# Two graph-attention layers on one core: row lists moved ahead, pair steps moved back, five adjacency gathers in flight

## What is computed

```python
# layer 0
att    = ((x[sub] @ Wq.T + bq) * (x[obj] @ Wk.T + bk)) summed over each of 8 heads / sqrt(64)
scores = zeros(8, n, n); scores[:, sub, obj] = att
scores = where(adj == 0, -inf, scores); scores[:, i, i] = 1e-07
x = layernorm(x + mean_over_heads(softmax(scores)) @ x)
# layer 1
seq = (x @ W_seq) in 16 heads
hidden = softmax(leaky_relu(s1[i] + s2[j]) masked by adj) @ seq
x = layernorm(x + elu(hidden @ W_out + b_out))
```

## Time and profile before

| what | value |
|---|---|
| median of 3 runs | 434.89 us (434.27 to 435.85) |
| the profiled execution's own time | 433.42 us |
| its span in the profile | 431.1 us |
| PE (TensorE) busy | 351.7 us, 82% |
| DVE (VectorE) busy | 323.1 us, 75% |
| ACT (ScalarE) busy | 202.1 us, 47% |
| POOL (GpSimd) busy | 186.5 us, 43% |

### The profile page before, as it was taken

The page is one execution under the profiler, slowest core; times in us unless marked ns, Lnnn a source line. Parts: engine busy times, 40 slices in busy tenths (PEclk is TensorE's granted clock), DMA queues, the critical chain, the costliest instruction groups (busy, mean ns, idle before and its releaser), DMA issues.

```text
span 431.1 us, 5195 instructions
## 1 busy us (share of the span) xinstructions
PE 351.7 (82%) x1650; PEld 214.2 (50%) x1650; DVE 323.1 (75%) x813; ACT 202.1 (47%) x451; POOL 186.5 (43%) x180
## 2 busy tenths in 40 slices
PE   1599999999600699979999999258898999999991
PEld 1155644544300354537887877036554565565650
DVE  0999799766500556977777785778799999999955
ACT  3867664476200021225564534211154477577684
POOL 6655767655367100000000000677778887884000
PEclk9999999999955699999999999578999999999997
DMA  7999144436940013219311111575666567666014
GB/s 263 380 390 378 37 176 126 156 112 161 276 123 0 6 48 74 99 25 365 120 58 52 68 59 52 154 216 140 176 190 187 153 198 225 180 201 193 24 51 152
DMA packets 34758, 65.11 MB, mean 151 GB/s; under 512 B 15648, under 2 KB 16800, under 8 KB 32672
## 3 DMA queue, kind: packets, MB, share of 16 engines
q1 hardware_dynamic: 25632, 42.45, 28.9%
q0 software_dynamic: 9088, 22.20, 18.8%
HBM read 53.50 MB, written 8.52 MB: 144 GB/s over the span
## 4 chain that ended last, share of the span: by engine, by line
DVE 32%; DMA 22%; PE 19%; POOL 15%; issue 7%; ACT 3%; another core or an unknown queue 0%; DVEq 0%; POOLq 0%; SPq 0%
DMA pr<-in_adj_dram,aidx 21%; PE ps L811 12%; POOL pr L524 8%; DVE adjT L1939 8%; POOL adjT L603 6%; PE ps L633 3%; DVE arenaC L1806 2%; DVE ps L1864 2%; DVE adjT L1804 2%; DVE ps L1857 2%; DVE arenaA L1870 2%; DVE stage L1929 2%; PE ps L800 2%; PE ps L671 2%; DMA adjT<-seqtab,eidx 1%
## 5 line engine op out<-in xcount | busy, mean ns | idle before, releaser
L633 PE MATMUL ps<-arenaB,adjT 128*128 128x512 f16 x512 | 120.2, 392 | 5.5 <-ACT adjT L982 3.2
L524 POOL DMA_INDIRECT pr<-in_adj_dram,aidx x79 | 83.1, 1051 | 52.5 <-DMA pr<-in_adj_dram,aidx 36.1
L603 POOL DMA_INDIRECT adjT<-seqtab,eidx x64 | 76.1, 1189 | 19.5 <-issue 19.5
L633 PEld LDWEIGHTS ps<-arenaB,adjT 128*128 128x128 f16 x512 | 50.2, 101 | 66.8 <-issue 6.3
L925 PE MATMUL ps<-adjT,stage 128*128 128x264 f32 x256 | 67.1, 409 | 18.5 <-DVE adjT L1939 11.5
L603 POOL DMA_INDIRECT adjT<-seqtab,near x16 | 21.2, 1322 | 126.2 <-DMA seqtab<-arenaA 120.3
L925 PEld LDWEIGHTS ps<-adjT,stage 128*128 128x128 f32 x256 | 48.8, 198 | 41.1 <-DVE ps L1864 16.5
L811 PE MATMUL ps<-stage 128*128 128x272 f32 x256 | 61.5, 394 | 0.2 <-ACT stage L1068 0.2
L838 PE MATMUL ps<-adjT 128*128 128x512 f32 x120 | 54.1, 593 | 1.0 <-issue 1.0
L811 PEld LDWEIGHTS ps<-stage 128*128 128x128 f32 x256 | 47.4, 190 | 9.6 <-ACT stage L1068 0.8
L1939 DVE TENSOR_TENSOR adjT<-adjT 128x1024 f32<-128x1024 f32 (+2 forms) x35 | 47.8, 1371 | 1.9 <-issue 1.3
(11 more groups left out here) (274 smaller groups left out, 507.6 us busy)
## 6 DMA issues: line engine op xcount, KB each, us to landing
stage<-in_adj_dram SPq DMA_DIRECT2D x16, 1024.0 KB
seqtab<-arenaA SPq DMA_DIRECT2D x16, 264.0 KB, 2.0
arenaA<-in_x_dram SPq DMA_DIRECT2D x4, 1024.0 KB, 12.1
out_dram<-arenaC SPq DMA_DIRECT2D x16, 256.0 KB
arenaB<-in_x_dram SPq DMA_DIRECT2D x1, 1536.0 KB, 10.4
pr<-in_adj_dram,aidx POOLq DMA_INDIRECT x79
arenaC<-in_L_gnn_Wq_dram SPq DMA_DIRECT2D x1, 1024.0 KB
arenaC<-in_L_gnn_Wk_dram SPq DMA_DIRECT2D x1, 1024.0 KB
```

The costliest lines, as they stand in the source:

```text
L524: g.indirect_dma_start(out=avals[:, t:t + 1], out_offset=None, in_=adj_flat, in_offset=bass.IndirectOffsetOnAxis(ap=aidx[:, t:t + 1], axis ...
L603: g.indirect_dma_start(out=Grow[:, b % GR, k, :], out_offset=None, in_=seqtab, in_offset=bass.IndirectOffsetOnAxis(ap=source, axis=0)).the ...
L633: ins = t.matmul(bank(4 + b % 2), adjT[:, b, j, :], xsplit[:, w, j, :], start=(j == 0 and w == 0), stop=(j == NB - 1 and w == 1))
```

## The change

- GpSimd: from gather 24 on (`CALM`) five may be in flight (`FLIGHT`), before it three as before. The mask `nearer` is made by VectorE at its start, and is 64 wide.
- TensorE: `pair_offsets` and `pair_list` move from block 11 to block 13, `pair_turn` and `pair_qk` from 12 to 14, `count_rows` and `pair_rows` ahead of block 15, `pair_sums` and `pe_sum_flags` to its middle. Blocks 0 and 1 are multiplied quarter by quarter side by side.
- VectorE: the list of block 13 is finished before `count_pairs`; those of 14 and 15 stand between `fetch_pairs` and the branch. In the arm, `all_listed` comes before `attend`, and `lone_rows` and `measure` before `weigh_pairs`. Block 0's list comes before the first `low`.
- ScalarE: the cast of block 15 moves ahead of the branch. SP: block 1 is loaded before the first quarter of `x`, block 2 before the last.
- The tables of the pair steps are 64 wide where they were 128 (at most 64 pairs are taken in this arm). `attend` waits for q and for k apart.

The diff, without its renamings:

```diff
-    FLIGHT = 3
+    FLIGHT = 5
+    CALM = 24
-        diag = part(stage, 2176, [10, P])
-        prod8 = part(stage, 2176, [H0, P])
+        diag = part(stage, 2176, [10, FEWER])
+        prod8 = part(stage, 2176, [H0, FEWER])
...
             load_row(0)
+            load_row(1)
             load_x(0)
-            load_row(1)
             load_x(1)
             load_x(2)
+            load_row(2)
             load_x(3)
-            load_row(2)
...
             for t in range(T):
-                if t >= FLIGHT:
-                    pool.wait_ge(c_av[t % FLIGHT], 16 * (t // FLIGHT))
+                ahead = FLIGHT if t >= CALM else 3
+                if t >= ahead:
+                    pool.wait_ge(c_av[(t - ahead) % FLIGHT], 16 * ((t - ahead) // FLIGHT + 1))
...
-                if b == 11:
+                if b == 13:
                     pair_offsets()
+                if b == 14:
+                    pair_qk()
                 multiply(b, 2 * Q, 3 * Q)
-                if b == 11:
+                if b == 13:
                     pair_list()
...
+            count_rows()
+            pair_rows()
             multiply(NB - 1, 0, Q)
             multiply(NB - 1, Q, 2 * Q)
             pe_sum_flags()
+            pair_sums()
+            multiply(NB - 1, 2 * Q, 3 * Q)
             pair_scatter()
-            multiply(NB - 1, 2 * Q, 3 * Q)
...
-            list_keys(NB - 3)
+            listing(NB - 3)
             count_pairs()
             place_pairs()
             fetch_pairs()
-            list_top(NB - 3)
+            listing(NB - 2)
+            listing(NB - 1)

             def last_rows():
-                listing(NB - 2)
+                all_listed()
                 attend()
-                listing(NB - 1)
-                all_listed()
-                weigh_pairs()
                 lone_rows()
                 measure()
+                weigh_pairs()
                 share_pairs()
                 weigh_rows()
```

More of the change, by code:

```diff
@@ L243, in two_layer_graph_attention @@
         pair_step = Stage(sem("pair_step"), ["tot", "hot8", "cur", "diag", "mx8", "akeep", "vsel"])
+        pair_pe = Stage(sem("pair_pe"), ["off", "list", "turn", "q", "k", "cnt", "rows", "bad", "sums", "scat"])
         A_dve = Stage(sem("A_dve"), [f"hot{c}" for c in range(NCH)] + ["shift", "so", "idx", "prod", "red", "att",
@@ L993, in _ @@
                 if q == 0:
-                    save_turned(0)
-                if q == 1:
-                    cast_row(1)
-            save_turned(1)
-            cast_row(2)
+                    save_turned(1)
+                if q == 2:
+                    cast_row(2)
+            save_turned(2)
+            for b in range(2):
+                save_ax(b)
+            cast_row(3)
             def block_step(b):
@@ L1011, in block_step @@
                         s.copy(WT[:, g // KT, g % KT, :], bank(6 + g % 2)).then_inc(w_evac_a, 1)
-                if b == 13:
-                    act.wait_ge(so_turned, 1)
+                if b == 14:
+                    act.wait_ge(pair_pe.sem, pair_pe.after(0, "turn"))
                     for w in range(2):
@@ L1017, in last_rows @@
             def last_rows():
-                for b in (NB - 2, NB - 1):
-                    block_step(b)
+                block_step(NB - 1)
+                act.wait_ge(pair_pe.sem, pair_pe.after(0, "rows"))
+                s.copy(Up[:], ps[:, 1, 0:P]).then_inc(u_saved, 1)
                 act.wait_ge(pair_step.sem, pair_step.after(0, "mx8"))
@@ L1025, in last_rows @@
                 save_ax(NB - 2)
-            for b in range(2, NB - 2):
+            for b in range(3, NB - 1):
                 block_step(b)
@@ L1346, in fetch_pairs @@
             def fetch_pairs():
-                dve.wait_ge(listed8, 1)
+                dve.wait_ge(pair_pe.sem, pair_pe.after(0, "list"))
                 link(v.tensor_scalar_add(cur[:, 0:2], ps[:, 7, 0:2], -1.0))
@@ L1448, in weigh_rows @@
                                        ALU.subtract).then_inc(fast_done, 1)
-                dve.wait_ge(bad_summed, 1)
+                dve.wait_ge(pair_pe.sem, pair_pe.after(0, "bad"))
                 v.tensor_copy(badi[:], ps[:, 3, 64:65]).then_inc(flag_made, 1)
-            for b in range(4):
-                low(b)
             dve.wait_ge(masks, 11)
+            v.tensor_copy(nearer[0:FEWER, :], before[0:FEWER, 0:FEWER])
+            v.tensor_copy(nearer[FEWER:P, :], before[FEWER:P, FEWER:P])
             link(v.tensor_scalar(offdiag0, identh[:], -1.0, 1.0, ALU.mult, ALU.add))
@@ L1457, in _ @@
             list_top(0, key0, top0, junk0)
-            for b in range(4, NB):
+            for b in range(NB):
                 low(b)
```

113 lines of the change are left out of this document (53 added, 60 removed).

## The result

The changed kernel takes 470.86 us (median of 4 runs, 465.48 to 473.25) against 434.58 for the kernel before: ratio 1.0792, 95% interval 1.0733 to 1.085. I had forecast 413.8 us, range 408 to 421, and 0.95 for faster. It is slower by 8%: outside the range, and on the other side.

The account below looks back on a forecast made before the run. The prediction took the landing of 79 gathers to bound the kernel's first third. Gathers 11.9 us earlier plus a 9.2 us shorter path to `fast_done` made 21.1 us less: 413.8 us, range 408 to 421.

Parts of the forecast that it names:

- term 2: TensorE before `pair_offsets`: two more blocks, 14.3 us, lie beside the gathers; it is ready at 129.6 and waits only 2 us.
- Term 1: GpSimd's gathers: with five in flight, landing waits fall from 16.0 to 2 us; values at 130.3 instead of 142.19, 11.9 us earlier.
- all waits go: Best bound for the gathers: all landing waits and all long issues vanish, values at 122.5.
- Term 3: VectorE's path from the gathered values to `fast_done`: reordered pair steps shorten 46.5 us to 37.3, 9.2 us less.
- More in flight does not help: Rival: landings, not depth, set the gathers' pace; values still at 142.2, 425.7 us in all; chance 0.12.
- TensorE becomes the bound: Rival: gathers reach their floor and `pair_offsets` waits for TensorE; 2 to 5 us better, 408.7 to 411.7; chance 0.15.
- The slower rival: Gathers fall to their starting pace of 1.97 us each; values at 161.5, 445.0 us in all; chance 0.03.
- Products hold an issue in full: Rival: each of nine VectorE products holds a gather issue 1.23 us, not 0.5; values at 136.9, 420.4 us; chance 0.08.

Follow-up runs that it names:

- e17: Changed kernel with a 64-element GpSimd fill after each of gathers 24 to 65, none after the last 13: 418.82 us against 433.33 for the kernel before.
- e14: Kernel before, its order kept, with five gathers in flight from number 24 on and a 160-element fill after each: ratio 0.999 to the kernel before.
- e13: Changed kernel with a 160-element GpSimd fill after each gather from number 24 on: ratio 0.989 to the kernel before.
- e1: Changed kernel with three gathers in flight throughout: ratio 0.996 to the kernel before.
- e2: Kernel before, its order kept, with five gathers in flight from number 24 on and three semaphores joined in one: ratio 1.068 to the kernel before.
- e10: Kernel before, its order kept, with five gathers in flight from number 24 on and a 64-element fill after each: 431 to 446 us.
- e15: Changed kernel with a 64-element GpSimd fill after each gather from number 24 on: ratio 0.978 to the kernel before.
- e6: Changed kernel with four fills and waits on GpSimd after each gather from number 24 on: ratio 1.090 to the kernel before.
- e11: Changed kernel with three gathers in flight throughout and a 64-element fill after each from number 24 on: 437.64 us, ratio 1.008 to the kernel before.
- e18: e17 with 32 more matmuls, result unused, before TensorE's wait for the pairs: ratio 0.970 to the kernel before.
- e16: Changed kernel with four 64-element fills after every fourth gather only, from number 24 on: ratio 0.989 to the kernel before.

## Why the prediction was wrong, by its steps

**The step that failed** is in term 2: "So these 14.3 us lie wholly beside the gathers", and behind it the whole sum, which lets every engine keep its pace while GpSimd's stream closes up. I had TensorE at `pair_offsets` at 129.6; it came at 187.06. Between 76 and 129 it did 16 matmuls of the product, and about 6 us were lost before. I priced a faster GpSimd for the issues that lengthen beside VectorE's products and for the DMA, and never asked whether the 16.0 us of waits that I took away were room that others used. The stretch that I read, 122.93 to 139.16, could not tell, since TensorE had nothing to do in it. But the trace of before holds another, with all engines at work, and in it the effect in small. TensorE's transposes, ScalarE's copy of them, and GpSimd:

```profile
68.08 1.06 PE L617 MATMUL ps<-identh,halves 128*128 128x128 f16 x16
68.72 1.93 ACT L982 COPY adjT<-ps 128x1024 f16<-128x1024 f16 x2 [3.49 <-PE ps L617]
...
75.88 1.06 PE L617 MATMUL ps<-identh,halves 128*128 128x128 f16 x16
78.13 1.93 ACT L982 COPY adjT<-ps 128x1024 f16<-128x1024 f16 x2 [5.09 <-PE ps L617]
...
78.75 0.94 POOL L524 DMA_INDIRECT pr<-in_adj_dram,aidx  x1 [2.35 <-DMA pr<-in_adj_dram,aidx]
```

The copy follows its transposes by 0.64 us at 68, and by 2.25 at 78, after ten gathers from 62.88 on with 0.30 us between them (one of them held for 2.26 us). It begins inside the next landing wait (76.39 to 78.75). The copy after it, at 86.61, is late and inside a landing wait as well.

**Term 1, the gathers.** Right about the landing waits: without one the last issue began at 119.33, near the 52.12 + 67.4 = 119.5 of "all waits go". But this is no test of the depth, since the loads that made the waits stood still. In e17, where the others run, the account can be checked: 49.39 + 79.04 (54 steps of 1.464) + 3.19 = 131.62, forecast 130.3. Against my terms: the start 2.7 us earlier (I had 0, and bounds of 3 either way), 42 fills of 0.14 us, 5.9 (not in the change), long issues 4.3 for 5.8, landing waits some 1.5 for 2. One reading was off: the long issues of before did not last "about until its end", the end of VectorE's product, but 0.8 us beyond it, all five, and the one at 52.12 was held 0.8 us, not 0.9; the sum hardly moves by it.

**Term 3, values to `fast_done`.** Forecast 37.3, and where there was no stall it is 40.9 to 43.4 (e14, the order before: 46.6). In e17, 41.9, three sizes were off, none in the mechanism: `curi` at +6.4 and not +5.1, since TensorE waited 8.34 us and not 2 and did its eight matmuls in 3.57 us at a granted clock of 0.50, as before (3.57 at 0.50, and 7.13 for the next 32 at 1.00, is what the prediction's slow clock and slow level are the earlier trace rows); VectorE's time before the branch 5.71 and not 3.60, 2.1 more; `pair_rows` 2.47 for 1.2, 1.2 more, right behind a wait of TensorE of 3.50 us and at a granted clock of 0.53 at 162 to 164; together 4.6.

```profile
160.00:162.00 2.00, 1.19 (x2) 0.71 (x3) 1.86 (x12) 0.00 (x0) 0.00 (x0) 0.62 0.00 0
162.00:164.00 2.00, 2.00 (x6) 1.01 (x6) 0.79 (x6) 0.27 (x1) 0.00 (x0) 0.53 0.02 4
```

In the changed kernel itself the tail is 51.5, of which 11.04 is the wait for TensorE. And "What comes behind is not touched by the change" was not quite so: the stretch from `fast_done` to the end is 241.7 to 243.1 us in the four profiles of the order before, and 242.4 to 246.2 in those of the changed one. Why is open.

**The sum without the failed step.** e17 keeps the change and adds only the pauses: values 10.6 us earlier (forecast 11.9), tail 4.6 shorter (9.2), 1.0 us given back behind `fast_done`, together 14.2 of the spans; 433.42 - 418.70 = 14.7 of the executions' own times. So two thirds of the forecast gain were there once the pauses were, behind a stall that I had not seen.

**The rivals.** "More in flight does not help" is refuted by e13 and e14 as far as waits go, and true as far as time goes in the order before. "TensorE becomes the bound" happened, for another reason. The slower rival had the wrong mechanism: the gathers did not slow down to 1.78 us a step, they sped up to 1.29. "Products hold an issue in full" did not happen: long issues cost 4.3 us, less than my middle value. The 2.22 us issue at 64.29 does stand beside a product (63.40 to 65.69), but no product explains the stall: TensorE was held while VectorE had nothing under way (77.0 to 131.2).

**Still open.** By what TensorE is held is not shown. The DMA's share of 0.02 and 0 GB/s exclude bandwidth. A late fetch of instructions was my next guess; the trace's DMA records speak against it. The trace marks some transfers as "instruction". Between the second and the third of those with 16 KB lie 280 records of TensorE (matmuls, weight loads, waits) in e1, 284 in e2, 286 in the changed kernel and 288 in before, though 22, 69, 83 and 23 us apart. So the third was not late by TensorE's own count. That the stall keeps itself up (nobody issues loads, so gathers land at once, so GpSimd never waits) is read from the traces and was not tried apart. Nor is it settled why VectorE's time before the branch is 3.60 and 3.40 us in before and e14, and 5.4 to 5.9 in all others; e2 (5.84) and e10 (5.71) have the order before, so it isn't the order. The DMA records narrow it: in each of the 20 profiles one "instruction" transfer of 8 KB begins in this idle time, 1.9 to 2.1 us before its end. It begins 1.5 us into it in before and e14, and 3.4 to 3.9 us in all others. What holds it back is open.

## What to carry to other kernels

A wait that looks like waste on one engine can be what lets the others run; before you remove it, look in the trace for a stretch in which that engine already runs without a pause *while the others have work*, and see whether anyone starts late there (here 62.88 to 76.39, and the copy at 78.13); if there is none, the effect is unpriced and belongs in the range. Widen a window of indirect DMAs together with a small pause, sized by a measurement (here 0.14 us a gather was enough in one order of the other engines' work and not in the other), and try dropping it for the last few. When a change turns out slower, look first for idle time released by "issue" or "remote", and follow it to the engine that the others wait for: here ScalarE's "remote" led back to TensorE.

## What the runs showed of the hardware that I had not expected

- Indirect DMAs of 128 elements issued each 1.25 us without a pause bring TensorE from 67 matmuls in 10 us to 6 and fewer, and ScalarE and VectorE, which wait for it, to nothing for some 50 us, at a DMA share of 0.02; at 1.39 us each they cost the others little or nothing in one order (339 matmuls in 60 us in e15, as many as at 2.3 us each in e6), and more in another (e10: 240 where e14 has 322).
- The hold shows first in what TensorE hands on: ScalarE's copy begins 0.04 us after the transposes where gathers rest (e11, e13 to e18, from about 50 us on), up to 1.9 us in before, up to 52 us in the changed kernel.
- A rest of 1.4 us after every fourth gather (e16, 1.52 us a gather in the mean) is as good as 0.5 us after each (e13, 1.47).
- The same branch costs VectorE 3.4 to 3.6 us in two kernels and 5.4 to 5.9 in the others, behind the same instructions that read the number of pairs; some 2.0 us of it lie behind an 8 KB transfer marked "instruction" in all of them.
